# A quad of heads' values product in one group at the end of the odd slot, in a layer kernel with attention and a feed-forward part

## The reference

```python
x = x + layernorm(attention(layernorm(x), w_qkv, b_qkv, w_out, b_out))
x = x + layernorm(relu(layernorm(x) @ W1 + b1) @ W2 + b2)

scores = q @ k.T / 4 + mask          # per head, 512 x 512
out    = softmax(scores) @ v         # per head, 512 x 16
```

## Time and profile before

| what | us |
|---|---|
| median of 3 runs | 2374.32 |
| lowest and highest | 2372.41, 2374.86 |
| span of the profiled execution, first to last instruction | 2371.9 |
| PE busy | 2296.9 (97%) |
| PE weight loads busy | 1917.6 (81%) |
| DVE busy | 1739.7 (73%) |
| ACT busy | 1487.9 (63%) |
| POOL busy | 781.8 (33%) |

### The profile page before, as it was taken

The page is one execution under the profiler, slowest core; times in us unless marked ns, Lnnn a source line. Parts: engine busy times, 40 slices in busy tenths (PEclk is TensorE's granted clock), DMA queues, the critical chain, the costliest instruction groups (busy, mean ns, idle before and its releaser), DMA issues.

```text
span 2371.9 us, 59261 instructions
## 1 busy us (share of the span) xinstructions
PE 2296.9 (97%) x18176; PEld 1917.6 (81%) x18176; DVE 1739.7 (73%) x3909; ACT 1487.9 (63%) x3077; POOL 781.8 (33%) x1159
## 2 busy tenths in 40 slices
PE   5899999999999999999999999999999999999997
PEld 3678888888888888888888888888888888888876
DVE  5777777777777777777777777777777777777742
ACT  3456666666666666666666666666666666666654
POOL 0023332333332333332333332333332333332344
PEclk8989999999999999999999999999999999999998
DMA  6444444344444444444344444444444444444410
GB/s 141 95 85 80 87 87 93 78 88 78 86 86 93 78 88 78 86 85 92 79 88 78 86 85 92 79 88 79 86 85 92 79 88 79 86 85 84 82 33 18
DMA packets 158659, 197.93 MB, mean 83 GB/s; under 512 B 37392, under 2 KB 88336, under 8 KB 158600
## 3 DMA queue, kind: packets, MB, share of 16 engines
q1 hardware_dynamic: 107400, 146.83, 34.4%
q10 hardware_dynamic: 51200, 50.34, 6.7%
HBM read 37.25 MB, written 16.78 MB: 23 GB/s over the span
## 4 chain that ended last, share of the span: by engine, by line
PE 88%; DVE 5%; DMA 3%; issue 2%; ACT 1%; POOL 1%; SPq 0%; DVEq 0%; POOLq 0%; ACTq 0%
PE p_lin L425 29%; PE p_lin L490 15%; PE p_max L359 8%; PE p_o L408 7%; PE p_sc L383 7%; PE p_max L354 6%; PE p_o L405 5%; PE p_sc L378 5%; PE p_lin L417 3%; DMA stack<-max_row 2%; PE p_lin L453 2%; DVE neg_max L646 2%; PE p_lin L438 1%; DVE max_row L677 1%; POOL h_lo L789 1%
## 5 line engine op out<-in xcount | busy, mean ns | idle before, releaser
L533 ACT ACTIVATE probs<-p_sc 128x512 f32<-128x512 f32 x1280 | 725.3, 603 | 590.4 <-PE p_sc L378 317.2
L646 DVE TENSOR_REDUCE neg_max<-p_max 128x2 f32<-128x512 f32 (+1 forms) x1280 | 856.0, 679 | 192.3 <-PE p_max L359 112.7
L789 POOL TENSOR_TENSOR h_lo<-h_f,h_hi 128x256 fp32r<-128x256 f32 x512 | 364.9, 732 | 512.1 <-ACT h_hi L571 505.9
L359 PE MATMUL p_max<-stack 72*128 72x256 f32 x1536 | 341.6, 304 | 19.5 <-DVE neg_max L646 19.2
L571 ACT ACTIVATE h_f<-p_lin,b_s 128x256 f32<-128x256 f32 x512 | 243.4, 475 | 120.7 <-PE p_lin L425 120.3
L359 PEld LDWEIGHTS p_max<-stack 72*128 72x128 f32 x1536 | 244.0, 191 | 89.6 <-issue 52.2
L383 PE MATMUL p_sc<-stack 80*128 80x256 f32 x1536 | 310.2, 284 | 0.0
L425 PE MATMUL p_lin<-x_hi,w_hi 128*128 128x256 f32 (+1 forms) x1280 | 297.3, 314 | 3.7 <-ACT h_hi L571 2.0
L490 PE MATMUL p_lin<-w_hi,h_hi 128*128 128x256 f32 x1024 | 292.6, 286 | 7.2 <-POOL h_lo L789 6.0
L383 PEld LDWEIGHTS p_sc<-stack 80*128 80x128 f32 x1536 | 273.8, 192 | 28.9 <-ACT probs L533 0.7
L490 PE MATMUL p_lin<-w_lo,h_hi 128*128 128x256 f32 x1024 | 291.2, 284 | 0.0
(11 more groups left out here) (81 smaller groups left out, 3767.2 us busy)
## 6 DMA issues: line engine op xcount, KB each, us to landing
stack<-qk SPq DMA_DIRECT2D x2048, 64.0 KB, 2.3
xa<-x ACTq DMA_DIRECT2D x32, 512.0 KB, 3.9
xr<-x ACTq DMA_DIRECT2D x32, 512.0 KB, 3.5
out<-yf ACTq DMA_DIRECT2D x64, 256.0 KB, 2.5
stack<-max_row SPq DMA_DIRECT2D x256, 32.0 KB
probs<-w SPq DMA_DIRECT2D x2, 512.0 KB, 4.7
probs<-w_qkv_t SPq DMA_DIRECT2D x2, 384.0 KB, 5.0
x_old<-w SPq DMA_DIRECT2D x1, 512.0 KB, 6.9
```

Source lines behind the costliest of these rows:

```text
L359: last = nc.tensor.matmul(dst[:, j * 2 * P:(j + 1) * 2 * P].rearrange("p (a n) -> p a n", a=2), q_stack[0:MAXROW, buf, j, kb * P:(kb + 1) ...
L533: nc.scalar.activation(probs[:, CH * (p % 2) + c, :], p_sc[k % 2][:, :], ACT.Exp, scale=SCALE).then_inc(exp_done, 1)
L646: nc.vector.tensor_reduce(dst, src, axis=AX.X, op=ALU.max, negate=True).then_inc(red_done, 1)
L789: last = nc.gpsimd.tensor_tensor(h_parts[1][:, m, :], h_f[:, n % 2, u, :], h_parts[0][:, m, :].bitcast(F32), ALU.subtract)
```

## The change

The values product of a quad moves: its key blocks 0 and 1 go from turn 2 of the odd slot to turn 4, in front of blocks 2 and 3. The matmuls, their operands and waits are the same. Nothing else in the program changes, on any engine.

```diff
-PV_TURNS = {2: (0, 1), 4: (2, 3)}
+PV_TURNS = {4: (0, 1, 2, 3)}
```

## The result

The changed kernel takes 2450.74 us (median of 4, 2449.1 to 2452.84) against 2374.59 us (median of 4) for the kernel before on the same chips: a ratio of 1.0325, 95% interval 1.031 to 1.0339. It is 76 us slower. The forecast was 2449.

What follows compares the result with a forecast made beforehand. The prediction took PE, busy in 97% of the span, as the bound. Slot terms 1.17 + 0.81 - 0.28 + 0.73 - 0.1 gave +2.33 us per sample, 74.6 us over 32, hence 2449 us; range 2412 to 2480.

Steps and rivals of the forecast that it cites:

- The removed change of shape: On PE, one switch fewer per quad between 128-column work and the product's 32-column work: -0.28 us per quad.
- Slot 3: PE's scores of turn 3 wait 0.98 us for max_row's DMA, plus 0.11 for weights; net +0.81 us.
- The estimate worked out from the Trainium skill's fit: DMA landing about 2.07 us after issue, not 2.38: both max_row waits 0.31 shorter, time 2429 us.
- Slot 7: max_row's DMA goes out late behind SP's eight stack loads; PE waits 0.90 us, weights 0.11, net +0.73 us.
- Slot 4: The bare wait for max_row may shrink as DVE has turn 3's statistics behind it earlier: -0.1 us.
- Slot 1: PE waits for turn 1's exponential, then for DVE's reduction of turn 2, held by ln1's four applications: +1.17 us.
- The exponentials' new wait: ACT's exponentials for the next quad wait for block 0's matmuls at turn 4; taken as zero, margin 0.2 us.
- The sum: Slots' terms add to +2.33 us per sample, times 32 is 74.6 us, on the median: 2449 us.
- the first samples: First and last samples, with less linear work around the slots, lose at least as much; not corrected for.
- Faster: Rival: PE is the bound, stalls don't come, only the changes of shape go: 2338 us; chance 4%.
- mildly slower: Rival: the two DMA waits come, but PE isn't held in slot 1: +1.0 us per sample, 2406 us; chance 10%.
- A: The half of a quad's values product with key blocks 0 and 1, at turn 2 of the odd slot before.

Runs made afterwards that it cites:

- slot5_only: Kernel before, with the values product joined in one group at turn 4 in slot 5 alone; 2365.33 us, ratio 0.996.
- Slot3_only: Kernel before, with the values product joined in one group at turn 4 in slot 3 alone; 2406.73 us, ratio 1.0126.
- sp_split: Changed kernel, with SP issuing the second four of slot 6's eight stack loads only after slot 7's max_row DMA; 2440.9 us, ratio 1.0279.
- all_at_turn3: Kernel before, with all four key blocks of the product at the end of turn 3 of the odd slots; 2492.57 us, ratio 1.0494.

## Why the prediction was right

**The removed change of shape** was sized at 0.28 per quad and is 0.34 (slot 5, and slot5_only). The mis-sized term is the split between the group's second half and its exit: I read 0.45 for eight short matmuls plus 0.1 of exit. With the joined group there are two lengths to compare: 24 took 1.41 us and 16 took 1.00, so eight are 0.41 and the exit is 0.18. The Trainium skill (TensorEngine Tiling (Array Packing), "Key Properties") has a drain at each change of tiling mode; the rows agree that each group costs something fixed: the exit comes out the same, 0.18, behind 16 and behind 24. What a drain is within that 0.34 the rows don't tell.

**Slot 3** was right in cause and size (wait 0.98 predicted, 0.99 measured). Slot3_only shows it as slot 3's own. The landing taken from slot 4's rows held: 2.41 in the chain. (The prediction counts them from DVE's end and so has 2.38 from the issue; the chain's entries, 1109.56 and here 1000.28, begin at SP's issue, 0.02 to 0.03 later. It changes nothing in the sum.) The estimate worked out from the Trainium skill's fit (DMA: Bandwidth & Descriptors, "Anatomy of one DMA"), 2.07 us from issue and 20 us less in all, did not come: the page gives it for the gpsimd path, this DMA is SP's, and the measurement decides.

**Slot 7** was right (0.90 against 0.91). SP's queue is the cause of 0.5 us of that wait, shown by sp_split; the rest is the DMA's own 2.4 us.

**Slot 4** was right in size and cause (0.1): DVE starts max_row 1.14 us into the slot (1008.49) in place of 1.25 (1037.75), and PE's scores of turn 3 come as much earlier.

**Slot 1** was right in size (1.17 against 1.12) and in the order of its waits, for the exponential first and then for DVE at turn 4. A third wait, of 0.43 for the reduction of (1, 1), it doesn't name; it ends before the exponential's and costs nothing. That the four applications on DVE were a fixed 2.35 was taken from the rows without asking why; it held only as long as POOL's addition stayed beside them.

**The exponentials' new wait** was costed at nothing, and cost nothing: in the steady state ACT's waits for block 0 delay PE nowhere, since PE's only wait for an exponential there is that of (1, 1), and all_at_turn3, which shortens ACT's wait, was slower. That block 0's wait costs exactly zero wasn't tried by itself.

**The sum** was better than its terms. The steady sample was put at +2.33 and is +2.08, which makes 8 us less over 32 samples; the terms that are off are the change of shape, four times 0.06. For the first samples I wrote that they lose at least as much, for having less linear work, and corrected nothing; they cost about 13 us more than steady ones, and that is a term the sum doesn't have: the lower granted clock at the start, where the prediction had 1.00 from one steady sample. Together that is 5 more than the forecast, and the span of the profiled execution shows it (79.1 more, against 74.6). That the medians are within 2 us of 2449 is in part luck: two errors of opposite sign.

**The rivals.** "Faster" needed the waits not to come, "mildly slower" an early slot 1; the rows above rule out both.

## What to carry to other kernels

Work placed between a producer's start and its consumer on the busy engine is a cover, and belongs to whoever waits behind it. Before moving it, list the waits of the next instructions and subtract each releaser's end from PE's new arrival: that gave each slot of the changed kernel to 0.1 us. Do it for the new place and for every old one: of the split product's halves each hid something, and where the half that moved hid nothing (A in slot 5) the join was a free 0.34 us. After removing a wait, look for the next producer with a margin smaller than what was gained (h_lo in sp_split). And compare the granted clock of the start by itself: a price read from one steady sample leaves out what the first ones lose.

## What the runs showed of the hardware, unexpected

A DVE tensor_scalar that runs SBUF to SBUF takes 0.41 us alone and up to 1.38 us when POOL's tensor_tensor of 1.3 to 1.4 us starts beside it. The POOL instruction itself took 1.29 us alone and 1.44 in the collision. The Trainium skill (SBUF — State Buffer, "Who interferes with whom") says that a DVE instruction in one of its two-port modes, which tensor_scalar can enter, shares a port pair with GpSimd, and that the first to issue holds the pair for the whole instruction while the other blocks. The trace agrees. POOL's addition starts at 1058.30, within the third of the four applications, and is 0.15 longer than alone; the fourth, which starts at 1058.52, bears the whole delay of 0.97 and ends 0.15 behind POOL's instruction.

The granted clock of the start depends on the order of PE's work: up to the fourth sample it was 0.91 before and 0.85 with the joined groups, for the same 1497 matmuls.
